# Router logits of the last two token blocks on GpSimd, ScalarE and the vector engine instead of TensorE

## What is computed

```python
x_rotated = hamilton(q_left_n, hamilton(ifft(fft(x_quat) * spectral_gate).real, q_right_conj))
probs = softmax(xf @ Wr.T, axis=-1)                       # 8 experts
h = gelu(xf @ W1[7] + b1[7], approximate=False)           # 256 -> 1024
y = (h @ W2[7] + b2[7]) * probs[:, 7:8]                   # 1024 -> 256
return x + y
```

## Time and profile before

| | us |
|---|---|
| median of 3 runs | 106.26 |
| lowest, highest of the 3 | 105.84, 348.34 |
| the profiled execution | 105.8 |
| its span on the core | 104.0 |
| TensorE busy | 100.1 |
| vector engine busy | 66.8 |
| ScalarE busy | 50.2 |
| GpSimd busy | 25.9 |

### The profile page before, as it was taken

The page is one execution under the profiler, slowest core; times in us unless marked ns, Lnnn a source line. Parts: engine busy times, 40 slices in busy tenths (PEclk is TensorE's granted clock), DMA queues, the critical chain, the costliest instruction groups (busy, mean ns, idle before and its releaser), DMA issues.

```text
span 104.0 us, 1511 instructions
## 1 busy us (share of the span) xinstructions
PE 100.1 (96%) x570; PEld 85.1 (82%) x570; DVE 66.8 (64%) x143; ACT 50.2 (48%) x83; POOL 25.9 (25%) x16
## 2 busy tenths in 40 slices
PE   7998999999999999999999999999999999999990
PEld 7887888888888888888888888888888878888980
DVE  1579689788274999298225996272494962378451
ACT  3285894544442484484414534944424544442700
POOL 3400000029999300000000000069998000000000
PEclk9999999999999999999999999999999999999999
DMA  2989990260004122440500050000005040000005
GB/s 67 325 265 316 222 181 1 53 152 3 0 0 150 61 109 93 97 108 0 202 0 0 0 208 0 0 0 0 0 0 202 6 202 0 0 0 0 0 10 191
DMA packets 10726, 8.38 MB, mean 81 GB/s; under 512 B 7904, under 2 KB 8544, under 8 KB 10720
## 3 DMA queue, kind: packets, MB, share of 16 engines
q1 hardware_dynamic: 10144, 7.51, 25.4%
q10 hardware_dynamic: 576, 0.79, 2.3%
HBM read 6.20 MB, written 2.10 MB: 80 GB/s over the span
## 4 chain that ended last, share of the span: by engine, by line
PE 92%; DVE 3%; ACT 1%; DVEq 0%; issue 0%
PE pre L661 40%; PE acc L668 25%; PE acc L676 15%; PE lT_bank L577 3%; PE lT_bank L620 2%; PE pre L631 2%; PE acc L672 1%; PE acc L670 1%; PE acc L583 1%; ACT xT_hi L302 1%; DVE y L491 1%; PE extra L602 1%; PE lT_bank L602 1%; DVE w_lo L424 1%; DVE xT_lo L408 1%; DVE xT L417 1%
## 5 line engine op out<-in xcount | busy, mean ns | idle before, releaser
L330 ACT ACTIVATE h_hi<-pre,quats 128x512 fp32r<-128x512 f32 x32 | 22.1, 690 | 43.4 <-PE pre L661 42.0
L457 DVE TENSOR_TENSOR h_lo<-h_all,h_hi 128x512 fp32r<-128x512 f32 x32 | 21.8, 689 | 20.6 <-ACT h_all L332 20.4
L668 PE MATMUL acc<-w_parts,h_hi 128*128 128x512 f32 x116 | 32.3, 391 | 0.0
L668 PEld LDWEIGHTS acc<-w_parts,h_hi 128*128 128x128 f32 x116 | 21.5, 188 | 4.5
L661 PE MATMUL pre<-xT_hi,w_hi 128*128 128x512 f32 x60 | 24.0, 400 | 0.0
L661 PE MATMUL pre<-xT_lo,w_hi 128*128 128x512 f32 x60 | 23.7, 395 | 0.0
L676 PE MATMUL acc<-w_parts,h_lo 128*128 128x256 f32 x128 | 23.0, 283 | 0.0
L278 POOL TENSOR_TENSOR exps<-e_const,shifted 128x32 f32<-128x32 f32 x4 | 22.3, 5578 | 0.2
L676 PEld LDWEIGHTS acc<-w_parts,h_lo 128*128 128x128 f32 x128 | 20.0, 189 | 2.7 <-DVE h_lo L457 0.7
L332 ACT ACTIVATE h_all<-pre,quats 128x512 f32<-128x512 f32 x32 | 21.8, 682 | 0.0
L661 PE MATMUL pre<-xT_hi,w_lo 128*128 128x512 f32 x60 | 18.7, 392 | 0.0
(11 more groups left out here) (75 smaller groups left out, 60.6 us busy)
## 6 DMA issues: line engine op xcount, KB each, us to landing
x_sq<-in_x SPq DMA_DIRECT2D x12, 128.0 KB, 3.6
x_in<-in_x SPq DMA_DIRECT2D x3, 512.0 KB, 3.2
out<-y SPq DMA_DIRECT2D x3, 512.0 KB, 2.7
w<-in_W SPq DMA_DIRECT2D x4, 256.0 KB, 4.5
x_in<-in_x SPq DMA_DIRECT2D x2, 256.0 KB, 4.9
w_rest<-in_W_rest SPq DMA_DIRECT2D x2, 256.0 KB, 3.3
w_first<-in_W_first ACTq DMA_DIRECT2D x1, 264.0 KB, 3.0
w_rest<-in_W_rest ACTq DMA_DIRECT2D x1, 256.0 KB, 4.1
```

Source lines behind the costliest of these rows:

```text
L330: nc.scalar.activation(h_hi[:, s, :], pre[f % 2][:, :], ACT.Gelu, bias=b1_cols[:, f:f + 1]).then_inc(h_hi_ready, 1)
L457: nc.vector.tensor_tensor(h_lo[:, s, :], h_all[:, s, :], h_hi[:, s, :].bitcast(F32), ALU.subtract).then_inc(h_lo_ready, 1)
L668: nc.tensor.matmul(acc[j][:, :], rows, w2_parts[:, f, :, :], start=(f == 0), stop=False)
```

## The change

Three things change.
- **Logits of blocks 2 and 3** (LATE = 2). x of both blocks is loaded early as rows of tokens, x_late. The router's columns are stored by GpSimd's DMA queue to a DRAM tensor of 2048 numbers and loaded back, the same 2048 to every partition, as wr_all. GpSimd multiplies x_late by them, one instruction of 128x2048 for each of the 8 tiles of 128 tokens (`late_product(n)`), into 4 buffers. Products 0, 1, 2, 4 and 5 are summed over the channels by ScalarE, with 8 activations each that have an accumulator output, in groups of four (`late_sums(n, half)`), placed behind Gelu of chosen tiles. Products 3, 6 and 7 are summed by the vector engine with one reduction each. Then follow the maximum (`late_maximum`, vector engine), and the subtraction and power (`late_softmax`, GpSimd).
- **The router on TensorE** remains for blocks 0 and 1 alone.
- **The opening.** The vector engine transposes the second half before it makes xT_lo of the first, and makes xT_lo of both halves before it splits w1's second chunk. TensorE does hi·hi and lo·hi of both halves first, and the products with xT_lo of both halves last.

```diff
             sp.wait_ge(x_turned, turned(0))
             load_squares(1)
+            for b in range(LATE, N_BLOCKS):
+                sp.dma_start(x_late[:, b - LATE, :, :], x_blocks[b]).then_inc(x_late_loaded[b - LATE], 16)
...
-                if b < LAST:
+                if b + 1 < LATE:
...
+            pool.wait_ge(wr_ready, KC)
+            nc.gpsimd.dma_start(wr_flat.rearrange("p (k e) -> p k e", k=KC), wr_wide[:, :, 0:NE]).then_inc(wr_stored, 16)
+            pool.wait_ge(wr_stored, 16)
+            nc.gpsimd.dma_start(wr_all[:, :, :].rearrange("p c e -> p (c e)"),
+                                wr_flat.rearrange("p n -> (p n)").unsqueeze(0).to_broadcast([P, C * NE])
+                                ).then_inc(wr_spread, 16)
+
+            def late_product(n):
+
+                if n >= PRODUCTS:
+
+                    pool.wait_ge(act_sums, ACT_DONE[n - PRODUCTS])
+                    pool.wait_ge(dve_sums, DVE_DONE[n - PRODUCTS])
+                pool.wait_ge(x_late_loaded[n // TT], 16)
+                nc.gpsimd.tensor_tensor(product[n % PRODUCTS][:, :, :],
+                                        x_late[:, n // TT, n % TT, :].unsqueeze(2).to_broadcast([P, C, NE]),
+                                        wr_all[:, :, :], ALU.mult).then_inc(product_ready, 1)
...
+            pool.wait_ge(wr_spread, 16)
+            late_product(0)
+            pool.wait_ge(max_ready, 1)
...
+            for n in range(1, TT + 2):
+                late_product(n)
+            late_softmax(LATE)
+            for n in range(TT + 2, 2 * TT):
+                late_product(n)
+            late_softmax(LAST)
...
+            def late_sums(n, half):
+
+                act.wait_ge(product_ready, n + 1)
+                for e in range(half * NE // 2, (half + 1) * NE // 2):
+                    nc.scalar.activation(product[n % PRODUCTS][:, :, e], product[n % PRODUCTS][:, :, e], ACT.Copy,
+                                         accum_out=logits_late[:, n // TT, n % TT, e:e + 1]).then_inc(act_sums, 1)
...
+            def late_sums(n):
+
+                dve.wait_ge(product_ready, n + 1)
+                nc.vector.tensor_reduce(logits_late[:, n // TT, n % TT, :],
+                                        product[n % PRODUCTS][:, :, :].rearrange("p c e -> p e c"),
+                                        AX.X, ALU.add).then_inc(dve_sums, 1)
+
+            def late_maximum(b):
+                n = TT * (b - LATE + 1) - 1
+                dve.wait_ge(act_sums, ACT_DONE[n])
+                dve.wait_ge(dve_sums, DVE_DONE[n])
+                nc.vector.tensor_reduce(late_max[:, :], logits_late[:, b - LATE, :, :], AX.X,
+                                        ALU.max).then_inc(late_max_ready, 1)
...
             for k in range(KC):
                 first_w1_low(k)
+            turn_first_x()
             first_x_low(0)
-            turn_first_x()
+            first_x_low(1)
             split_w1(1)
-            first_x_low(1)
...
-                    if b % 2 == 0 and f == 4:
-                        router(b // 2)
+                    if b == 0 and f == 4:
+                        router(0)
```

More of the change, by code:

```diff
@@ L57, in adaln_ffn @@
     N_QUAT = 4 + 16 + 1
+    LATE = 2
+    PRODUCTS = 4
     WARM_UP = 7
@@ L129, in adaln_ffn @@
         inv_sum = sb("inv_sum", [P, TT])
+        x_late = sb("x_late", [P, N_BLOCKS - LATE, TT, C])
+        wr_all = sb("wr_all", [P, C, NE])
+        wr_flat = nc.dram_tensor("wr_flat", [P, KC * NE], F32).ap()
+        product = [sb(f"product{i}", [P, C, NE]) for i in range(PRODUCTS)]
+        logits_late = sb("logits_late", [P, N_BLOCKS - LATE, TT, NE])
+        late_max = sb("late_max", [P, TT])
+        late_shifted = sb("late_shifted", [P, TT, NE])
         prob = sb("prob", [P, TT])
@@ L211, in turned @@
             return KC * (b + 1)
+        BY_ACT = (0, 1, 2, 4, 5)
+        ACT_DONE = [sum(NE for m in BY_ACT if m <= n) for n in range(2 * TT)]
+        DVE_DONE = [sum(1 for m in range(n + 1) if m not in BY_ACT) for n in range(2 * TT)]
         def store(engine, j):
@@ new lines, in _ @@
+            pool.wait_ge(wr_spread, 16)
+            late_product(0)
+            pool.wait_ge(max_ready, 1)
+            nc.gpsimd.tensor_tensor(shifted[:, :, :], logits,
+                                    logit_max[:, :].unsqueeze(2).to_broadcast([P, 2 * TT, NE]),
+                                    ALU.subtract).then_inc(shifted_ready, 1)
+            pool.wait_ge(shifted_ready, 1)
+            for i in range(2):
+                nc.gpsimd.tensor_tensor(exps[i][:, :, :], e_const[:, :].unsqueeze(2).to_broadcast([P, TT, NE]),
+                                        shifted[:, i * TT:(i + 1) * TT, :], ALU.pow).then_inc(exps_ready, 1)
@@ L644, in opening @@
                         products(w1_lo, xT_hi, half, f)
-                    pe.wait_ge(first_xT_lo_ready, KC * (half + 1))
-                    for f in range(2):
+                for f in range(2):
+                    for half in range(2):
+                        pe.wait_ge(first_xT_lo_ready, KC * (half + 1))
                         last = products(w1_hi, xT_lo, half, f, ends=(half == 1))
-                        if half == 1:
-                            last.then_inc(pre_done, 1)
+                    last.then_inc(pre_done, 1)
             def first_product(b, f):
```

65 lines of the change are left out of this document (52 added, 13 removed).

## The result

The changed kernel takes 129.9 us (median of 4 runs, 128.05 to 131.91) against 106.4 us for the kernel before on the same chip. The ratio is 1.213, 95% interval [1.2065, 1.2189]: slower by over 22 us. 105.3 us was forecast, with a range of 104.3 to 109.5. The profiled execution of the changed kernel took 130.6 us, its span 128.8.

A forecast was written before the change was run, and what follows sets the result against it. TensorE, 92% of the chain, was taken to bound the kernel. Router -1.25, opening +0.15 and block 3's wait +0.2 gave -0.9 us: 104.9 on the profiled execution, 105.3 as the median forecast, range 104.3 to 109.5.

The forecast's parts named there:

- The router on TensorE: Router product of blocks 2 and 3 leaves TensorE, shortening its path: -1.25 us.
- Rival B: A GpSimd product keeps the vector engine's two-input instructions out while it runs: 109.7 us, or 116 with 4.5 us products; chance 0.15.
- The product: One GpSimd multiplication of 128x2048 takes 2.7 us; up to 5.8 us it costs nothing.
- The sum on ScalarE: Each accumulating activation behind Gelu takes 0.40 to 0.45 us and costs nothing; TensorE waits from about 0.50 us.
- The sum on the vector engine: Each of three reductions of 128x2048 takes 2.4 us, between 2.3 and 5.0; block 3 loses 0.2 us.
- rival A: Slower sums on ScalarE (+1.9), longer vector reductions (+1.0 and +1.2) or a late first softmax (up to +2.1); chance 0.19.
- The first softmax: On GpSimd behind two transfers and product 0, ready 18.1 to 25.8: costs nothing, upper end 2.1 us.
- The opening: Reordered start on the vector engine and TensorE: its end moves by +0.15 us.
- with a late x_sq: Case of the opening where x_sq's landing limits the transposes: its end moves by +0.4 us.
- The wait of block 3: The reduction and the maximum stand between two h_lo in block 3: 0.2 us lost.
- The sum: All terms together, -1.25 + 0.15 + 0.2 = -0.9 us, giving a forecast of 105.3 us; chance 0.55.

The follow-up runs named there:

- e2: The kernel before with the router of blocks 2 and 3 left out on TensorE: 104.75 us, ratio 0.9878.
- e3: The changed kernel with whole products stored expert by expert, so that every sum reads 256 neighbours: 119.9 us, ratio 1.1313.
- e5: The kernel of e3 with GpSimd's products cut to 32 of the 256 channels: 106.0 us, ratio 0.9996.
- e4: The kernel before with GpSimd multiplications, memsets and a copy added whose results nobody uses: 111.87 us in a single execution.
- e6: The changed kernel, sums still strided, with GpSimd's products cut to 32 of the 256 channels: 119.6 us, ratio 1.1283.
- e10: The kernel before plus the router columns' two transfers, the x_late loads and one product ahead of the first softmax: 109.76 us, ratio 1.0228.
- e1: The kernel before with the opening's two reorderings and nothing else: 106.54 us, ratio 1.0041.
- e7: The changed kernel with GpSimd's product 0 behind the first softmax instead of ahead of it: 131.15 us, ratio 1.236.
- e9: The kernel of e3 with each product cut into four GpSimd instructions of 64 channels: 121.7 us, ratio 1.1369.
- e11: The kernel before with only block 3's logits off TensorE, products on the vector engine, contiguous sums on ScalarE: 105.92 us, ratio 0.9963.

## Why the prediction was wrong

**The router on TensorE: right.** -1.25 us was taken from the two periods; e2 gave -1.3, of which its trace shows 1.11 in block 2.

**Rival B was ruled out by a row that did not bear on it: the main error.** It was given 0.15, with a price of up to 116 for a product of 4.5 us. The step that failed is "Against it": h_lo at 27.52 ran in 0.69 us beside a pow. A pow of 32 numbers does not hold the vector engine (the row stands, and in the change too h_lo ran at its usual length beside the pows), but a multiplication of 2048 numbers does, and so does a copy. The prediction had even said "those read 32 elements each, not 2048", and then let the row decide. The sentence of the Trainium skill's page SBUF — State Buffer, section "Who interferes with whom", was right for these instructions; the rows beside the pows do not fit it, and why is open. With contiguous sums, whole products instead of short ones cost 13.9 us (e3, e5). The mechanism was as B had it: one two-input instruction between two products. B had added its whole 0.69 us to the product; measured, a product takes 3.77 us alone and they start 4.2 apart with an h_lo between them.

**The product.** 2.7 us was taken, the measured mean is 4.0 (3.8 to 4.2). The two pow rows gave a fixed part of 0.67 us and the subtraction of 64 the rest, 1.0 ns an element. Two lengths of this very product, 759 ns for 256 numbers (e5) and 4180 for 2048 (e3), give 1.9 ns an element and some 0.3 us fixed. The 4497 ns of the Trainium skill's page GPSIMD Engine Reference, section "Performance versus the Vector engine", is nearer (e4: 4.60 for the first one). By the prediction's own rule a length up to 5.8 us costs nothing; no run shows long products without the hold, so that rule was not tested.

**The sum on ScalarE.** 0.40 to 0.45 us was taken, "nothing" as the price, from 0.50 on waits. Measured: 0.70 from start to start when strided, and 0.40 when contiguous, the reading of the accumulator included (e3, e5). That range was bounded by a copy of neighbours (0.36); the step of 8 numbers was not priced here, though it was seen for the vector engine. So the estimate was right for a layout that the kernel did not have; e5 shows that such sums do fit.

**The sum on the vector engine.** 2.4 us was chosen between 2.3 and 5.0, "the pace of long streams". Contiguous, it is 2.28; strided, as written, 4.16. The row set aside, lane_eye, was the nearer one, since it was the only strided row. Strides of both engines together cost 13.6 us (e5, e6); rival A had named both terms, with prices of 1.9 and 2.2. How this divides between ScalarE and the vector engine was not tried apart; the 3.9 us period of a tile is ScalarE's.

**The first softmax.** The transfers were bounded at 23.1 and ended at 23.83, the product at 27.6: beyond the upper end in both (in e10 21.99 and 25.7, just inside). It was costed at nothing, with 2.1 as the upper end; alone it costs 2.4 us (e10). In the change block 0 lost 4.1: the stop of 3.79, and 0.4 of the opening. The lower clock from 38.2 on lies behind block 0's end; what it costs in block 1, where h_lo is held anyway, was not tried apart.

**The opening.** +0.15 was taken, +0.4 measured (e1). That is the case "with a late x_sq", which was named: the transposes could begin only at 7.22.

**The wait of block 3: right.** +0.2 was taken for a reduction of 2.4 us; in e5, with 2.28, the stretch to the end is 24.96 instead of 24.67.

**The sum.** Even without hold and stride the change is worth nothing: e5 is at 0.9996. The 1.3 us of the router go into the opening (0.4), block 3's wait (0.3) and a reduction in block 2 (22.61 against 22.38 in e2); the remaining 0.4 lie in block 0, and which part of the start takes them was not tried apart.

## What to carry to other kernels

Before work is moved to GpSimd, list what the vector engine does beside it that has two SBUF inputs: beside a multiplication or a copy each such instruction waited for the GpSimd instruction that was running, and here neither a reordering (e7) nor smaller pieces (e9) removed that. Let the writer choose the layout that the reader wants, since the sums took 70 to 80% longer with the stride and the product 4% longer. And a row only bounds a cost if it is of the same kind; a short pow says nothing about a long multiplication.

## What the runs showed of the hardware

- GpSimd and the vector engine take turns: while GpSimd has products queued, exactly one two-input instruction gets in after each, be the product 4.1 us (e3) or 1.3 us long (e9). Beside a pow of 32 numbers, 5.6 us long, h_lo keeps its 0.69 us.
- A CAST with one SBUF input took 4.01 us beside product 0 (23.91) and 0.39 to 0.46 before. The same section of the Trainium skill's page says that copies and casts in a two-port mode contend too, and that a reduction does not; the sum of exponentials at 55.99 in e9 took its usual 0.17 us beside a piece.
- Strided by 8 numbers, an activation of 256 numbers takes 711 to 754 ns instead of 417, and a reduction of 2048 takes 4.03 to 4.16 us instead of 2.28. The GpSimd product hardly minds the layout of its output: 4006 ns when it writes number after number (the change), 4180 when it writes at a step of 256 numbers (e3).
- The 8 KB store of the columns, whose pieces are 32 bytes long, took 5 us of waiting, and the load that spreads the same 2048 numbers to all partitions 7.2 us. The load varies: 5.3 us in e10, 5.1 in e11.
- After a stop of 3.79 us TensorE's granted clock fell to its lower level for about 3 us. So it did after stops of 2.45 us (the change, 93.04), 2.26 (e3, 36.21) and 1.95 (e4, 45.18), but not after 2.45 (e3, 88.34), 1.86 (the change, 67.20) and 1.75 (e10, in the profiled execution). The length of the last stop alone does not tell.
